# Six landing places for transposed score blocks, one output accumulator, the bias on GpSimd and the first masks on ScalarE, in the attention stage of a four-stage graph kernel

## The chip, the core and the metric

The kernel runs on one core of a Trainium2 chip. Its time is the device time of one execution in microseconds. The kernel before took 1704.58 us, the median of three runs (1696.35, 1704.58 and 1709.76). Engines are named as in the profile: PE is TensorE, PEld its weight loads, DVE is VectorE, ACT is ScalarE, POOL is GpSimd, SP is SyncE; SPq, ACTq and POOLq are the instructions with which these engines issue DMAs.

## What is computed

The input x has 3327 rows of 256 numbers, adj is a 3327 by 3327 matrix of zeros and ones. Four blocks follow one another, each added to x: an attention over the graph, a mixture of 8 experts with two chosen per row, a graph convolution, and a second mixture of experts. The change lies in the first block and in the projections ahead of it:

```python
def _L0_gnn_ref(x, adj, weight, bias, node_w, edge_w):
    node_att = jax.nn.softmax(x @ node_w, axis=0)
    h = x @ edge_w
    e = h @ h.T
    e = jnp.where(adj > 0, e, NEG_BIG)
    edge_att = jax.nn.softmax(e, axis=1)
    combined_att = node_att * edge_att
    support = x @ weight
    output = adj * combined_att @ support
    return output + bias
...
x = x + _L0_gnn_ref(_layernorm(x, axis=-1), adj, ...)
```

The product h h^T is symmetric, and both kernels use that.

## The kernel before, in words

Rows are worked on in tiles of 128, 26 of them (T = 26, padded to 3328 rows). Every engine has its own instruction stream, written out by hand tile by tile, and the streams meet at semaphores (`wait_ge`, `then_inc`). Nothing reorders them.

**Projection** (`project`). For each tile t, DVE normalises the rows (L511), PE transposes them (L564), ACT copies the transpose out (`copy_t`, L542), and PE multiplies by weight and node_w (L574) and by edge_w (L579). ACT then writes the high part of each product (support L550, h_t L551), and DVE the low part, the rest after rounding (L523, L525). All large products are kept as such pairs, high and low, and a product is formed from three partial products: high by high, high by low, low by high. In this stage SP also loads the first two rows of tiles of adj into one place ADJ (`adj_tile`), and POOL makes from each an additive mask, 0 or minus a large number, for tiles 0 and 1 (L492).

**Attention** (`attend`). For tile t:

- *Scores.* PE forms 7 chunks of up to 512 columns in an order (`ORDER`) that begins with the chunk of the tile itself. A chunk on or right of the diagonal is computed from `attn_h_tile` (HS, the tile's slice of h_t that POOL copies, L737) and h_t by six matmuls (L921). Those right of the diagonal are also copied out by ACT (L768) and stored to DRAM by SP (`raw_scores`, L658), and a chunk left of the diagonal is not computed: SP loads the stored block (L669) to one of `TURN_SLOTS` places and PE transposes it in four pieces (L916). Tile t has t // 4 such turned chunks, so five in tiles 20 to 23 and six in tiles 24 and 25. A place may be loaded again when PE has transposed what was in it: `load_scores(m)` waits for block m - `TURN_SLOTS`. DVE adds the mask and takes the maximum of each chunk (L828), which frees one of the four score banks. DVE is in order: in tile t's step its first five L828 of tile t + 1 stand ahead of the first two L811 of tile t.
- *Softmax.* ACT takes the exponential over the whole row tile (L781).
- *Output product.* PE transposes the probabilities (L930) in groups of four blocks; ACT writes their high part (L791), DVE the low part (L811). For each of 26 blocks PE multiplies the high part by support's high and low part at once, 512 columns (L956, L961 in the last block), and the low part by support's high part, 256 columns (L958). The left half of the bank holds two partial products, the right half one.
- *Tail.* DVE adds the bias to x (L865), adds the right half (L869), adds the left half (L872), and takes statistics (L226, L231). POOL normalises the new rows (L245 to L257), and a small gate is computed among the next tile's work.

PE's stream in step t is: scores of tile t + 1 with the first transposes of tile t set in after the fifth chunk, then the output product of tile t.

SP's stream in step t is: load adj for tile t + 1 (when POOL has made the mask out of ADJ, L742), store the output of tile t - 2 (L650), store its neighbour's normalised rows (L261), load x of tile t (L701), store kept chunks (L658), load turned chunks (L669), both for coming use.

ACT issues the first expert's weights for the next stage (`first_w_in`, `first_w_out`, L775 and L776) at tile 3; their places FIRST and FIRST_OUT are not read before the expert stage.

## Time and profile before

| what | value |
|---|---|
| time, median of 3 runs | 1704.58 us (1696.35 to 1709.76) |
| time of the profiled execution | 1700.52 us |
| its span, first to last instruction | 1698.7 us |
| granted clock of TensorE, mean | 0.949 |
| PE busy | 1480.6 us, 87% of the span |
| DVE, ACT, POOL busy | 1025.2, 660.3, 811.4 us |
| projection stage, about | 0 to 88 us of the span |
| attention stage, about | 89 to 650 us of the span |

The profiled execution lies 1.8 us outside its span (1700.52 against 1698.7) and 4.1 us below the median of the three runs. The busy time of PE counts instructions that overlap by their drain: the time from the start of one matmul to the start of the next is shorter than the duration of one. Shares over the whole span mix stages that have different limits, so places are read from the timeline, where the idle time ahead of an instruction and what ended it stand in square brackets.

### The profile page before, as it was taken

The numbers are of one execution on the slowest core, as the hardware profiler recorded it, in microseconds if no ns is written. First come the engines' busy times: TensorE is split into PE (matmuls) and PEld (weight loads), VectorE is DVE, ScalarE is ACT, GpSimd is POOL, SyncE is SP. The second block draws the span as 40 slices with busy tenths as digits, with TensorE's granted clock in tenths as the row PEclk, the third lists the DMA queues.
The fourth block names the chain that finished last, engine by engine and source line by source line (L and its number), as shares of the span: only waits on it lengthen the run. The fifth ranks groups of instructions, "written<-read, shape, count | busy, mean of one in ns | idle before, by whom it ended". The sixth has DMA issues, their size and how long they took to land. (4 is left out here: it accounts for less than half of the span.)

```text
span 1698.7 us, 35416 instructions
## 1 busy us (share of the span) xinstructions
PE 1480.6 (87%) x9072; PEld 1243.8 (73%) x9072; DVE 1025.2 (60%) x3475; ACT 660.3 (39%) x1483; POOL 811.4 (48%) x1578
## 2 busy tenths in 40 slices
PE   5889999999999874999989917899949999999994
PEld 4768788888888763778877804455538888888894
DVE  5546566677776664555565454677756655666652
ACT  2334444444443331222222332111125565555562
POOL 1013444444544424666666612688844445545551
PEclk8999999999999996999999969899969999999997
DMA  5056667666776522663323367888526632222223
GB/s 194 0 181 209 217 208 231 225 223 229 241 249 209 171 75 79 151 140 58 49 49 46 50 146 166 164 173 173 113 85 155 161 75 37 37 37 37 37 39 97
DMA packets 247532, 221.57 MB, mean 130 GB/s; under 512 B 120363, under 2 KB 226729, under 8 KB 243929
## 3 DMA queue, kind: packets, MB, share of 16 engines
q1 hardware_dynamic: 213784, 161.71, 34.2%
q0 software_dynamic: 25984, 31.06, 11.3%
q10 hardware_dynamic: 7680, 27.84, 4.4%
q8 instruction: 33, 0.54, 0.1%
q14 instruction: 51, 0.42, 0.1%
HBM read 127.29 MB, written 74.52 MB: 119 GB/s over the span
## 5 line engine op out<-in xcount | busy, mean ns | idle before, releaser
L1167 PE MATMUL bank<-ffn_w_in_parts,ffn_x_t 128*128 128x512 f32 x1416 | 363.1, 404 | 17.3 <-DVE ffn_x_t L1283 14.2
L1167 PEld LDWEIGHTS bank<-ffn_w_in_parts,ffn_x_t 128*128 128x128 f32 x1416 | 259.0, 190 | 77.1 <-DVE ffn_x_t L1283 17.5
L1191 PE MATMUL bank<-ffn_w_out_parts,ffn_hidden_t 128*128 128x256 f32 x2124 | 284.5, 288 | 16.8 <-DVE ffn_hidden_t L1290 16.5
L1191 PEld LDWEIGHTS bank<-ffn_w_out_parts,ffn_hidden_t 128*128 128x128 f32 x2124 | 262.9, 192 | 22.4 <-issue 15.8
L956 PE MATMUL bank<-support,attn_probs_t 128*128 128x512 f32 x650 | 254.8, 424 | 11.9 <-DVE attn_probs_t L811 11.6
L1131 POOL DMA_INDIRECT x<-ffn_y,ffn_dst x118 | 192.4, 1631 | 55.1 <-issue 52.8
L1486 PE MATMUL bank<-normed_parts,nbr_adj_t 128*128 128x512 f16 x676 | 161.6, 385 | 41.0 <-DVE nbr_adj_t L1605 36.0
L1233 ACT ACTIVATE ffn_silu_or_gelu<-bank,w_b_in 128x128 f32<-128x128 f32 x472 | 134.6, 368 | 145.2 <-PE bank L1178 145.2
L791 ACT CAST attn_probs_t<-bank 128x512 fp32r<-128x512 f32 (+1 forms) x182 | 98.9, 559 | 235.4 <-PE bank L930 233.2
L958 PE MATMUL bank<-support,attn_probs_t 128*128 128x256 f32 x676 | 188.9, 286 | 0.0
L811 DVE TENSOR_TENSOR attn_probs_t<-bank,attn_probs_t 128x512 fp32r<-128x512 f32 (+1 forms) x182 | 116.2, 651 | 96.5 <-ACT attn_probs_t L791 91.1
L1290 DVE TENSOR_TENSOR ffn_hidden_t<-ffn_silu_or_gelu,ffn_hidden_t 128x512 fp32r<-128x512 f32 x118 | 80.6, 692 | 126.2 <-ACT ffn_hidden_t L1239 120.1
L956 PEld LDWEIGHTS bank<-support,attn_probs_t 128*128 128x128 f32 x650 | 126.3, 194 | 38.7 <-issue 11.3
L828 DVE CUSTOM_DVE_ANT_0 attn_scores<-bank,attn_mask 128x512 f32<-128x512 f32 (+1 forms) x182 | 113.4, 649 | 57.8 <-PE bank L921 38.9
L921 PE MATMUL bank<-h_t,attn_h_tile 128*128 128x512 f32 (+1 forms) x660 | 143.1, 372 | 4.1 <-POOL attn_h_tile L737 4.1
L1486 PEld LDWEIGHTS bank<-normed_parts,nbr_adj_t 128*128 128x128 f16 x676 | 65.0, 101 | 107.2 <-issue 40.7
L921 PEld LDWEIGHTS bank<-h_t,attn_h_tile 128*128 128x128 f32 x660 | 117.4, 190 | 27.4 <-issue 4.2
L245 POOL TENSOR_TENSOR attn_rstd<-attn_mean_var,attn_constants 128x1 f32<-128x1 f32 x26 | 4.9, 188 | 272.6 <-DVE attn_mean_var L231 272.6
L958 PEld LDWEIGHTS bank<-support,attn_probs_t 128*128 128x128 f32 x676 | 131.6, 195 | 1.2
L1120 POOL DMA_INDIRECT ffn_x_gathered<-xn,ffn_tok x118 | 123.5, 1047 | 17.2 <-issue 1.2
L930 PE MATMUL bank<-attn_identity,attn_scores 128*128 128x128 f32 x676 | 102.4, 278 | 1.5 <-ACT attn_scores L781 1.5
L1130 POOL TENSOR_TENSOR ffn_wait_taker<-ffn_identity 128x1 f32<-128x1 f32 x118 | 23.3, 198 | 157.6 <-DVE ffn_y L1341 126.2
(274 smaller groups left out, 2561.0 us busy)
## 6 DMA issues: line engine op xcount, KB each, us to landing
adj_tile<-in_adj SPq DMA_DIRECT2D x25, 1663.5 KB
mask<-attn_mask ACTq DMA_DIRECT2D x26, 832.0 KB, 3.4
attn_scores_to_turn<-raw_scores SPq DMA_DIRECT2D x72, 256.0 KB
...
```

The source lines that it names most:

```text
L811: dve.tensor_tensor(PT[:, half(slot, g), 1, 0:gn * P], bank[4 + half(slot, g)][:, 0:gn * P], PT[:, half(slot, g), 0, 0:gn * P].bitcast(F32 ...
L828: dve.tensor_tensor_reduce(out=SC[:, slot, c0:c0 + cn], in0=bank[k % 4][:, 0:cn], in1=NEG[:, slot, c0:c0 + cn], scale=1.0, scalar=-3.0e38, ...
L921: ins = pe.matmul(bank[k % 4][:, 0:cn], HS[:, slot, hs, kd, :], HT[:, hm, kd, c0:c0 + cn], start=n == 0 and kd == 0, stop=n == 2 and kd == ...
L930: ins = pe.transpose(bank[4 + half(slot, g)][:, j * P:(j + 1) * P], SC[:, slot, (g0 + j) * P:(g0 + j + 1) * P], ID[:])
L956: pe.matmul(bank[6 + slot][:, :], part[:, 0, :], SUP[:, jt, :, :].rearrange("p a d -> p (a d)"), start=jt == 0, stop=False)
L958: ins = pe.matmul(bank[6 + slot][:, 0:D], part[:, 1, :], SUP[:, jt, 0, :], start=False, stop=False)
L1120: pool.indirect_dma_start(out=XG[:, slot, :], out_offset=None, in_=a["xn"], in_offset=bass.IndirectOffsetOnAxis(ap=TOKS[:, slot:slot + 1], ...
L1131: pool.indirect_dma_start(out=acc, out_offset=bass.IndirectOffsetOnAxis(ap=DSTS[:, slot:slot + 1], axis=0), in_=YS[:, slot, :], in_offset= ...
L1167: ins = pe.matmul(bank[2 + 2 * slot + b][:, :], XT[:, slot, xp, k, :], WIP[:, wp, k, b * CH:(b + 1) * CH], start=n == 0 and k == 0, stop=n ...
L1191: ins = pe.matmul(bank[7][:, 0:D], HTT[:, hp, k, :], WOP[:, wp, k, :], start=n == 0 and k == 0, stop=n == 2 and k == KH - 1)
L1233: ins = act.activation(GATE[:, j, k * P:(k + 1) * P], src[:, k * P:(k + 1) * P], ACT.Gelu, bias=w.BI[:, bass.ds(e * KH + (4 * j + k), 1)])
L1486: ins = pe.matmul(bank[2 + slot][:, :], AT[:, slot, g0 + j, :], XH[:, g0 + j, :, :].rearrange("p a d -> p (a d)"), start=g0 + j == 0, stop ...
```

## The change

It does six things.

1. `TURN_SLOTS` goes from 4 to 6. The places are no longer a tile of their own: they are FIRST (four places of 512 columns) and FIRST_OUT (two). So the first expert's weights can't be loaded until the last scores are formed, and their load moves from tile 3 to the last tile, behind `act.wait_ge(qk_done, T * NC)`.
2. The output product of one block is three matmuls of 256 columns into the same half bank, where it was one of 512 and one of 256 into a whole bank. DVE's L869 goes.
3. The addition of the bias moves from DVE (L865) to POOL (`add_bias`), and SP waits for it before it loads x again into the same place.
4. The masks of tiles 0 and 1 are made by ACT in the projection stage, as an activation over 3328 columns at tiles 17 and 23, where POOL made them. The second load of adj waits for the first mask as before, and so comes later.
5. POOL copies the h slices of tiles 0 and 1 in the projection stage, and PE waits for neither at the start of the attention.
6. The node softmax on POOL stands ahead of the tile steps; its small tiles have places of their own.

```diff
@@ -68,7 +68,7 @@
 ORDER = [list(range(t // 4, NC)) + list(range(t // 4)) for t in range(T)]
 KEPT = [(t, c) for t in range(T) for c in ORDER[t] if c > t // 4]
 TURNED = [(t, c) for t in range(T) for c in ORDER[t] if c < t // 4]
-KEEP_SLOTS, TURN_SLOTS = 3, 4
+KEEP_SLOTS, TURN_SLOTS = 3, 6
...
@@ -442,6 +443,7 @@
         projected, hi_ready, lo_ready = s.sem("projected"), s.sem("hi_ready"), s.sem("lo_ready")
 
         AT_STEP = {1: 1, 8: 2}
+        MASK_AT = {17: 0, 23: 1}
         with nc.Block(no_gpsimd_drain=True) as block:
             @block.sync
             def _(sp):
@@ -449,6 +451,7 @@
                 load_nodes(sp, X, a["x"], arrived)
 
                 sp.wait_ge(arrived[-1], 48)
+                sp.wait_ge(edge, 1)
                 sp.dma_start(a["ADJ"][:, 0:N], a["adj"][0:P, :]).then_inc(adj_in, 16)
                 sp.wait_ge(mask_made, 1)
                 sp.dma_start(a["ADJ"][:, 0:N], a["adj"][P:2 * P, :]).then_inc(adj_in, 16)
@@ -484,12 +487,13 @@
...
-
                 pool.memset(a["ADJ"][:, N:NP], 0.0).then_inc(edge, 1)
-                pool.wait_ge(edge, 1)
+                pool.memset(MINUS[:], -BIG).then_inc(edge, 1)
+
                 for t in range(2):
-                    pool.wait_ge(adj_in, (t + 1) * 16)
-                    pool.tensor_scalar(a["NEG"][:, t, :], a["ADJ"][:], BIG, -BIG, ALU.mult, ALU.add).then_inc(mask_made, 1)
+                    pool.wait_ge(lo_ready, (t + 1) * 2)
+                    pool.tensor_copy(a["HS"][:, t, :, :, :].rearrange("p a k n -> p (a k) n"),
+                                     HT[:, :, :, t * P:(t + 1) * P].rearrange("p a k n -> p (a k) n").bitcast(F32))
 
             @block.vector
             def _(dve):
@@ -546,6 +550,12 @@
                     slot = t % 2
                     if t + 1 < T:
                         copy_t(t + 1)
+                    if t in MASK_AT:
+
+                        m = MASK_AT[t]
+                        act.wait_ge(edge, 2)
+                        act.wait_ge(adj_in, (m + 1) * 16)
+                        act.activation(a["NEG"][:, m, :], a["ADJ"][:], ACT.Identity, bias=MINUS[:], scale=BIG).then_inc(mask_made, 1)
...
@@ -592,16 +602,18 @@
     HT, SUP, NL = a["HT"], a["SUP"], a["NL"]
     with ExitStack() as ctx:
         s = Stage(nc, ctx, "attn")
-
-        TURN = s.sb("scores_to_turn", [P, TURN_SLOTS, CH])
-        NATT, VAL, NSM = NL, TURN[:, 0, 0:T], TURN[:, 0, T:T + 4]
+        NATT, VAL, NSM = s.sb("node_attention", [P, T]), s.sb("valid", [P, T]), s.sb("node_small", [P, 4])
+
+        TURN = [v[:, i:i + CH] for v in (a["FIRST"][:].rearrange("p k m -> p (k m)"), a["FIRST_OUT"][:].rearrange("p k d -> p (k d)"))
+                for i in range(0, v.shape[1], CH)]
+        assert len(TURN) == TURN_SLOTS
...
-        HS = s.sb("h_tile", [P, 2, 2, KD, P], F32R)
+        HS = a["HS"]
...
@@ -694,6 +706,8 @@
                         store(t - 2, slot)
                     if t >= 3:
                         gate.store(sp, t - 3, 1 - slot)
+                    if t >= 2:
+                        sp.wait_ge(x_ready, t - 1)
...
@@ -729,25 +743,38 @@
                     pool.wait_ge(e_ready, 1)
                     pool.partition_all_reduce(NSM[:, 3:4], NSM[:, 2:3], P, RADD).then_inc(sum_all, 1)
 
+                def add_bias(t):
+
+                    slot, uses = t % 2, t // 2
+                    pool.wait_ge(x_in[slot], (uses + 1) * 16 + (16 if t == T - 1 else 0))
+                    if t >= 2:
+                        pool.wait_ge(x_out[slot], uses * 16)
+                        pool.wait_ge(gate.normed, t - 1)
+                    pool.tensor_tensor(XO[:, slot, :], XB[:, slot, :], BB[:], ALU.add).then_inc(x_ready, 1)
+
                 def step(t, uses, slot, first, last):
-                    if not known(t) or t >= 3:
+                    if t >= 3:
                         gate.norm(pool, t - 3, uses - 2 + slot, 1 - slot)
+                    if t >= 1:
+                        add_bias(t - 1)
                     if not first:
                         pool.wait_ge(masked, (t - 1) * NC)
-                    pool.tensor_copy(HS[:, slot, :, :, :].rearrange("p a k n -> p (a k) n"),
-                                     HT[:, :, :, bass.ds(t * P, P)].rearrange("p a k n -> p (a k) n").bitcast(F32)).then_inc(h_ready, 1)
+                        pool.tensor_copy(HS[:, slot, :, :, :].rearrange("p a k n -> p (a k) n"),
+                                         HT[:, :, :, t * P:(t + 1) * P].rearrange("p a k n -> p (a k) n").bitcast(F32)).then_inc(h_ready, 1)
                     if not first:
                         pool.wait_ge(adj_in, (t - 1) * 16 + (16 if last else 0))
                         pool.wait_ge(mask_out[slot], uses * 16)
                         pool.tensor_scalar(NEG[:, slot, :], ADJ[:], BIG, -BIG, ALU.mult, ALU.add).then_inc(mask_ready, 1)
-                    if first and slot == 1:
-                        node_softmax()
                     if t >= 4:
                         gate.scatter(pool, t - 4, uses - 2, slot)
                 gate.constants(pool)
+                node_softmax()
+                pool.wait_ge(bias_in, 16)
                 unrolled(T, step)
                 for t in range(T - 3, T):
                     gate.norm(pool, t, t // 2, t % 2)
+                    if t == T - 3:
+                        add_bias(T - 1)
                     gate.scatter(pool, t - 1, (t - 1) // 2, (t - 1) % 2)
...
@@ -771,7 +798,8 @@
                     if first and slot == 0:
                         act.wait_ge(nmx_ready, 1)
                         act.activation(NATT[:], NL[:], ACT.Exp, bias=NSM[:, 1:2], accum_out=NSM[:, 2:3]).then_inc(e_ready, 1)
-                    if known(t) and t == 3:
+                    if last:
+                        act.wait_ge(qk_done, T * NC)
                         act.dma_start(a["FIRST"][:], a["w_in"][0][:, :, 0:2 * H0]).then_inc(first_in, 16)
                         act.dma_start(a["FIRST_OUT"][:], a["w_out"][0][:, :, 0:D]).then_inc(first_in, 16)
...
@@ -858,17 +886,9 @@
                     dve.wait_ge(factor, t * 2 + 1)
                     dve.scalar_tensor_tensor(SM[:, slot, 5:6], SM[:, slot, 4:5], SM[:, slot, 3:4],
                                              NATT[:, bass.ds(t, 1)], ALU.mult, ALU.mult).then_inc(factor, 1)
-                    dve.wait_ge(x_in[slot], (uses + 1) * 16 + (16 if last else 0))
-                    if not first:
-                        dve.wait_ge(x_out[slot], uses * 16)
-                        dve.wait_ge(gate.normed, t - 1)
-                    dve.tensor_tensor(XO[:, slot, :], XB[:, slot, :], BB[:], ALU.add).then_inc(x_ready, 1)
                     dve.wait_ge(factor, t * 2 + 2)
                     dve.wait_ge(pv_group, (t + 1) * NG)
                     dve.wait_ge(x_ready, t + 1)
-                    dve.scalar_tensor_tensor(XO[:, slot, :], bank[6 + slot][:, D:2 * D], SM[:, slot, 5:6],
-                                             XO[:, slot, :], ALU.mult, ALU.add).then_inc(out_part, 1)
-                    dve.wait_ge(out_part, t + 1)
                     dve.scalar_tensor_tensor(XO[:, slot, :], bank[6 + slot][:, 0:D], SM[:, slot, 5:6],
                                              XO[:, slot, :], ALU.mult, ALU.add).then_inc(out_ready, 1)
...
             @block.tensor
             def _(pe):
                 def scores(t, slot, first, midway=None):
-                    pe.wait_ge(h_ready, t + 1)
+                    if t >= 2:
+                        pe.wait_ge(h_ready, t - 1)
...
@@ -952,14 +972,9 @@
                         for j in range(gn):
                             jt = g0 + j
                             part = PT[:, half(slot, g), :, j * P:(j + 1) * P]
-                            if jt < T - 1:
-                                pe.matmul(bank[6 + slot][:, :], part[:, 0, :], SUP[:, jt, :, :].rearrange("p a d -> p (a d)"),
-                                          start=jt == 0, stop=False)
-                            ins = pe.matmul(bank[6 + slot][:, 0:D], part[:, 1, :], SUP[:, jt, 0, :],
-                                            start=False, stop=False)
-                            if jt == T - 1:
-                                ins = pe.matmul(bank[6 + slot][:, :], part[:, 0, :], SUP[:, jt, :, :].rearrange("p a d -> p (a d)"),
-                                                start=False, stop=True)
+                            for n, (hp, hs) in enumerate([(0, 0), (0, 1), (1, 0)]):
+                                ins = pe.matmul(bank[6 + slot][:, 0:D], part[:, hp, :], SUP[:, jt, hs, :],
+                                                start=jt == 0 and n == 0, stop=jt == T - 1 and n == 2)
                         ins.then_inc(pv_group, 1)
...
@@ -1717,6 +1732,7 @@
             a["FIRST_OUT"] = layer.enter_context(nc.sbuf_tensor("first_w_out", [P, H0 // P, D], F32))
             with ExitStack() as keep:
                 a["ADJ"] = keep.enter_context(nc.sbuf_tensor("adj_tile", [P, NP], F32))
+                a["HS"] = keep.enter_context(nc.sbuf_tensor("attn_h_tile", [P, 2, 2, KD, P], F32R))
```

PE, within one group of the output product (`support` is the value operand, `attn_probs_t` the transposed probabilities). Before:

```order
L930 MATMUL bank<-attn_identity,attn_scores 128x128 x4
L956 MATMUL bank<-support,attn_probs_t 128x512
L958 MATMUL bank<-support,attn_probs_t 128x256
L956 MATMUL bank<-support,attn_probs_t 128x512
L958 MATMUL bank<-support,attn_probs_t 128x256
L956 MATMUL bank<-support,attn_probs_t 128x512
L958 MATMUL bank<-support,attn_probs_t 128x256
L956 MATMUL bank<-support,attn_probs_t 128x512
L958 MATMUL bank<-support,attn_probs_t 128x256
```

and now:

```order
L950 MATMUL bank<-attn_identity,attn_scores 128x128 x4
L976 MATMUL bank<-support,attn_probs_t 128x256 x12
L950 MATMUL bank<-attn_identity,attn_scores 128x128 x4
L976 MATMUL bank<-support,attn_probs_t 128x256 x12
L282 MATMUL bank<-attn_gate_w,attn_x_normed_t 128x8 x2
```

The eight matmuls of a group, 3072 columns in all, are twelve with the same number of columns; the place of the transposes is the same.

SP, the steps around the first tile with five turned chunks. Before:

```order
L658 DMA raw_scores<-attn_scores_kept 128x2x128
L669 DMA attn_scores_to_turn<-raw_scores 128x512 x4
L692 DMA adj_tile<-in_adj 128x3327
L650 DMA x<-attn_x_out 128x256
L261 DMA xn<-attn_x_normed 128x256
L701 DMA attn_x<-in_x 128x256
L658 DMA raw_scores<-attn_scores_kept 128x2x128
L669 DMA attn_scores_to_turn<-raw_scores 128x512 x5
```

and now:

```order
L670 DMA raw_scores<-attn_scores_kept 128x2x128
L681 DMA first_w_out<-raw_scores 128x512 x2
L681 DMA first_w_in<-raw_scores 128x512 x3
L704 DMA adj_tile<-in_adj 128x3327
L662 DMA x<-attn_x_out 128x256
L261 DMA xn<-attn_x_normed 128x256
L715 DMA attn_x<-in_x 128x256
L670 DMA raw_scores<-attn_scores_kept 128x2x128
```

Before, four blocks of the next tile are loaded a step ahead and the fifth stands in the step that needs it; now all five are loaded a step ahead.

ACT, the start of the last tile's step. Now:

```order
L819 CAST attn_probs_t<-bank 128x256
L803 DMA first_w_in<-in_w 128x2x1024
L804 DMA first_w_out<-in_w 128x4x256
L807 DMA mask<-attn_mask 128x3328
L809 ACTIVATE attn_scores,attn_small<-attn_scores,attn_small 128x3328
```

Before, the two loads of the first weights stood at this place of tile 3's step, and the last tile's step had only the store of the mask ahead of the exponential.

## Rows read from the trace of the kernel before

**Rows 1.** Busy time by stretch: PE, PEld, DVE, ACT, POOL (counts), granted clock, DMA share, GB/s

```profile
400.00:500.00 100.00, 97.79 (x646) 86.89 (x645) 74.33 (x319) 46.44 (x71) 46.74 (x95) 1.00 0.70 238
```

**Rows 2.** Waits in the attention: engine, line, waited for: us in total, times, longest

```profile
PE bank L916 <- DVE attn_max L828: 7.2, 5, 2.1
PE bank L916 <- DMA attn_scores_to_turn<-raw_scores: 7.1, 3, 2.9
```

**Rows 3.** Timeline of SP's queue, stores of the tiles' outputs: start, us, queue, line

```profile
173.22 0.34 SPq L650 DMA_DIRECT2D x<-attn_x_out  x1
...
200.52 0.34 SPq L650 DMA_DIRECT2D x<-attn_x_out  x1
...
221.63 0.34 SPq L650 DMA_DIRECT2D x<-attn_x_out  x1
...
496.05 0.34 SPq L650 DMA_DIRECT2D x<-attn_x_out  x1
...
515.07 0.34 SPq L650 DMA_DIRECT2D x<-attn_x_out  x1
...
619.49 0.34 SPq L650 DMA_DIRECT2D x<-attn_x_out  x1
```

**Rows 4.** Timeline of PE, late attention: start, us, line, count, [idle before <-releaser]

```profile
501.33 0.63 PE L916 MATMUL bank<-attn_identity,attn_scores_to_turn 128*128 128x128 f32 x4 [1.88 <-DMA attn_scores_to_turn<-raw_scores]
520.60 0.63 PE L916 MATMUL bank<-attn_identity,attn_scores_to_turn 128*128 128x128 f32 x4 [2.12 <-DVE attn_max L828]
```

**Rows 5.** Busy time by stretch, right behind the second of these gaps

```profile
520.60:523.60 3.00, 3.00 (x14) 2.67 (x15) 1.07 (x6) 0.00 (x0) 2.68 (x5) 0.65 0.72 221
```

**Rows 6.** Timeline of ACT, tile 3's exponential, behind three DMA issues

```profile
171.87 3.08 ACT L781 ACTIVATE attn_scores<-attn_scores,attn_small 128x3328 f32<-128x3328 f32 x1 [1.64 <-issue]
```

**Rows 7.** DMA issues: KB each, us from issue to landing

```profile
first_w_in<-in_w ACTq DMA_DIRECT2D x1, 1024.0 KB, 6.2
```

**Rows 8.** Groups by line: busy us, mean ns | idle before

```profile
L865 DVE TENSOR_TENSOR attn_x_out<-attn_x,attn_bias 128x256 f32<-128x256 f32 x26 | 10.9, 419 | 0.0
...
L869 DVE SCALAR_TENSOR_TENSOR attn_x_out<-bank,attn_small,attn_x_out 128x256 f32<-128x256 f32 x26 | 12.6, 484 | 4.0 <-PE bank L961 0.7
...
L257 POOL TENSOR_SCALAR attn_x_normed<-attn_x_out,attn_rstd 128x256 f32<-128x256 f32 x26 | 14.5, 558 | 0.0
```

**Rows 9.** Timeline of PE in an output-product group: second block, and what follows the fourth

```profile
448.18 0.40 PE L956 MATMUL bank<-support,attn_probs_t 128*128 128x512 f32 x1
...
449.23 0.60 PE L930 MATMUL bank<-attn_identity,attn_scores 128*128 128x128 f32 x4
```

**Rows 10.** Timeline of PEld: weight loads of the experts' 256-column matmuls, back to back

```profile
1430.36 2.94 PEld L1191 LDWEIGHTS bank<-ffn_w_out_parts,ffn_hidden_t 128*128 128x128 f32 x24
```

**Rows 11.** The same weight loads as a group by line

```profile
L1191 PEld LDWEIGHTS bank<-ffn_w_out_parts,ffn_hidden_t 128*128 128x128 f32 x2124 | 262.9, 192 | 22.4 <-issue 15.8 <-DVE ffn_hidden_t L1290 6.2
```

**Rows 12.** Timeline of ACT, DVE and PE in the projection stage, tiles 22 to 25

```profile
81.61 0.39 ACT L542 COPY proj_normed_t<-bank 128x256 f32<-128x256 f32 x1
...
82.22 0.41 DVE L511 TENSOR_SCALAR proj_normed<-proj_x,proj_mean_var 128x256 f32<-128x256 f32 x1
82.86 0.38 PE L564 MATMUL bank<-proj_identity,proj_normed 128*128 128x128 f32 x2
83.06 0.37 ACT L550 CAST support<-bank 128x256 fp32r<-128x256 f32 x1 [1.06 <-PE bank L579]
...
84.83 1.03 PE L574 MATMUL bank<-proj_weight_node,proj_normed_t 128*128 128x257 f32 x4
```

**Rows 13.** Timeline of POOL: the second mask, and how long it waited for adj

```profile
33.23 2.97 POOL L492 TENSOR_SCALAR attn_mask<-adj_tile 128x3328 bf16<-128x3328 f32 x1 [7.41 <-DMA adj_tile<-in_adj]
```

**Rows 14.** Timeline at the start of the attention

```profile
89.28 0.29 POOL L719 TENSOR_SCALAR_AFFINE_SELECT attn_identity<-attn_identity 128x128 f32<-128x128 f32 x1
...
90.82 2.41 PE L921 MATMUL bank<-h_t,attn_h_tile 128*128 128x512 f32 x6 [4.06 <-POOL attn_h_tile L737]
```

**Rows 15.** Timeline of PE behind the last tile's exponential

```profile
619.72 1.09 PE L930 MATMUL bank<-attn_identity,attn_scores 128*128 128x128 f32 x8 [1.54 <-ACT attn_scores L781]
```

18 lines of the change are left out of this document (9 added, 9 removed).

## The prediction, made before the changed kernel ran

> **What bounds the kernel now.** I read the busy time by stretch first, for the limit of the stage that is changed. In the middle of the attention PE is busy 97.8 of 100 us at full granted clock (1.00, the 2.4 GHz level), DVE 74, ACT and POOL under 47, and the DMA engines 70% at 238 GB/s [rows 1]. So there a term counts only if it is PE's own time, or lets PE wait. Next I read the waits, for PE's. The turned chunks (L916) account for two of them: 7.2 us in 5 waits put down to DVE and 7.1 us in 3 put down to the load of turned blocks [rows 2]. Third, the stores of the tiles' outputs, since the distance between two is the length of one tile's step [rows 3]: 19.02 us from 496.05 to 515.07, then 104.42 us for five steps (515.07 to 619.49), 20.9 each, although each holds less work for PE. Steps 19 and on are the first in which tiles 20 to 25, with five and six turned chunks, are scored. The gaps stand in PE's timeline [rows 4].
>
> **Six places.** With four places the fifth block of a tile can be loaded only when PE has transposed the first of the same tile. The gap at 501.33 is that, 1.88 us. The one at 520.60 (2.12 us) is put down to DVE, but it has the same place in the step and nearly the same length; I read it as the same load. Behind it the granted clock is 0.65 over 3 us [rows 5], after PE had stood; behind the 1.88 us no such loss appears. What a clean step would last comes from the first: 19.02 - 1.88 = 17.14 us. With six turned chunks one chunk of six 512-column matmuls, about 0.23 us each by the pair cost below, gives way to four transposes of about 0.45 us together (0.63 with their drain [rows 4]), so 0.9 us less: 16.2 us. The six steps lose 1.88 + (104.42 - 3 x 17.14 - 2 x 16.2) = 1.88 + 20.6 = 22.5 us, of which the clock is a third.
> All blocks are now loaded one step ahead, and the wait for the place is for the block six back. What is late next is DVE: five L828 and one L811 must be done before the output product starts, and L811 also waits for ACT's L791. I put 0.3 us of new gap in each step, 1.7 us in all. Gain: 20.8 us. Bounds: 14 us, if DVE's wait takes a gap of over 1 us in each step; 22.5 if none.
>
> **The first weights.** Their load at tile 3 (1.5 MB) meets the stores of kept chunks and the load of adj: the step that ends at 200.52 takes 27.30 us, the next 21.11 [rows 3]. Both hold the same scores but for one chunk's place. Gone: 6.2 us, bounds 3.5 and 6.2. At their new place ACT issues both ahead of the last exponential. At tile 3 this held ACT 1.64 us [rows 6]. PE waits for the last exponential already, 1.54 us [rows 15], so all 1.64 us add to a wait that becomes 3.2 us, and gaps that long have cost about 1.5 us of clock more (the step at 520.60: 20.9 - 17.14 - 2.12). Cost 3.1 us, bounds 1.6 and 3.3. Landing takes 6.2 us [rows 7] and has the whole last step as cover; without it the next stage would start later by the rest.
>
> **Bias and tail.** DVE loses L865 and L869, 0.419 + 0.484 = 0.9 us a tile [rows 8]. In most steps PE doesn't wait for DVE, so of 23.5 us nearly nothing shows: 0.5 us in the steps up to 19, and the 0.48 us of L869 behind the very last product. In the late steps it is what keeps the new gap at 0.3 us. Gain 1.0 us, bounds 0 and 3. POOL gains an addition of 128x256: between 0.56 us (L257, one operand) and twice that, since it reads two; it stands between the normalisation and the copy of h. POOL is under half busy [rows 1], and the sum of a tile is needed more than a step later. If that cover were gone, DVE would stand at the tail in every tile by what is missing. The mask and the next adj load move back by the same 0.6 to 1.1 us. SP's new wait is for an addition done a step before.
>
> **One accumulator.** Columns are the same, matmuls are 3 in place of 2. From 448.18, the second block of a group, to 449.23, the transposes behind the fourth, PE issues three blocks [rows 9], so 0.350 us a block. What a 256-column matmul with its own weight load costs is seen in the experts: 24 loads in 2.94 us, the last lasting 0.19, so (2.94 - 0.19) / 23 = 0.1196 us from one to the next [rows 10, 11]. Three make 0.359 us, 0.009 more than now; 26 x 26 blocks give +6.0 us, all on PE. Bounds: 0, if a third matmul costs its columns alone, and +10.
> The Trainium skill ("TensorE: Matmul & The Clock Gate", Back-to-back issue gap) states N / 2.4 + 2.5 ns for an isolated matmul; by that the third instruction would cost 2.5 ns and this term +1.7 us; rows 9 and 10, at the same clock, show larger gaps and decide.
>
> **First masks and h slices.** ACT waits 1.06 us per tile for PE in the projection. A mask is an activation over 3328 columns like the exponential, 3.08 us [rows 6]. Behind `copy_t`, which ends at 82.00, it lasts to 85.1 where ACT would start L550 at 83.06: 2.0 us late [rows 12]. Tile 17 has the same pattern; there the lateness goes through DVE to its normalisation of a later tile, which is ready at 82.63 for a transpose at 82.86, a slack of 0.2: PE stands 1.8 us. At tile 23 no normalisation is left; the copy for tile 25, one step of 2.0 us behind the one that ends at 82.00 and 2.0 late, is there at 86.0, where its matmul began at 84.83: 1.2 us. Cost 3.0 us, bounds 2 and 4. The second load of adj needed 7.4 us [rows 13] and has 10.6 us of cover (from the end of the first mask, six steps ahead of 85.1, to 82.0 + 1.8); if it were later, ACT would wait for the rest. At the start of the attention PE no longer waits for the h slices but for the identity, ready at 89.57 in place of 90.82 for the first matmul [rows 14]: gain 1.2 us. The node softmax is bound by the same waits as before: nothing.
>
> **Sum.** -20.8 - 6.2 - 1.0 - 1.2 = -29.2; +3.1 + 6.0 + 3.0 = +12.1; together -17.1 us. The profiled execution took 1700.5 us, so it would be 1683.4; the median of before is 4.1 us higher, and the forecast goes by the median: 1704.6 - 17.1 = 1687.5 us. Less than 1% (17.0 us) is about what can't be told from no change here.
>
> **Rivals.**
> *A: the third weight load is not hidden.* Loads last 192 ns [rows 11], longer than the 107 ns in which 256 columns stream at full clock. If a load were exposed in full, a 256-column matmul would cost 0.19 us and a block 0.58: +0.226 x 676 = 153 us, 1834 us. The rest of the change gives 29.2 - 6.1 = 23.1 us, 0.034 a block, so this decides from (0.350 + 0.034) / 3 = 0.128 us a matmul on, and makes it slower by 1% from 0.136 on. Rows 10 speak against it: 0.1196 with a different weight in each.
> The Trainium skill (same page, Measured speedup vs the span model) says of packed matmuls that a weight load overlaps a running matmul only when the row group differs; by that, with its 128 / 1.2 = 107 ns a load, a block would cost 0.65 us against 0.54 as an estimate, +74 us; rows 10 disagree, and I give it 2 in 100 within this rival. Chance of A together: 0.04.
> *B: the waits move.* The late steps become bound by DVE: seven L828 and two L811 stand between the tail and the start of the product. For it: PE's gap at 520.60 is put down to DVE. Against it: DVE has 26% of idle time, and gets 0.9 us a tile. Then the six places give 12 us and the rest stays: 1696 us. Chance 0.22.
> *C: the sum without the price of the third matmul*, a block costing as before, and the masks mostly hidden: -17.1 - 6.0 - 2 = -25, 1680 us. For it: in rows 9 the gap per instruction is nearly that small. Chance 0.20.
> *D: the change doesn't do what it says at tile 3*: the step is long for another reason (adj and kept chunks alone), or POOL's additions collide with the late adj load. Then 6.2 us stay: 1694 us. Chance 0.10.
> The forecast: 0.44.
>
> **Numbers.** The range takes in B, C and D and the spread of three runs: 1676 to 1701 us. Faster by over 1% means below 1687.5: half of the forecast's case (0.21), nearly all of C (0.19), a little of D and B: 0.45. Slower by over 1%: A and mishaps in the projection: 0.06. The same: 0.49.
>
> **What would show it.** Stores of outputs 17.4 and 16.5 us apart in the last six steps, no L916 wait over 0.5 us put down to DMA, granted clock near 1 there; a step of 21 us at tile 3; in the product twelve matmuls of a group in 1.43 us plus the entry; two PE gaps of 1.8 and 1.2 us in the projection; a gap of 3.2 us before the last exponential's transposes. It is wrong if blocks of the product cost over 0.37 us, if PE waits over 1 us for L828 or L811 in late steps, or if the step at tile 3 stays at 27 us.

## The result, and the profile after

The changed kernel takes 1687.4 us (median of 4 runs, 1685.0 to 1690.5) where the kernel before takes 1702.2 beside it (median of 4, one run more than in the table above). The record's ratio of the runs is 0.9898 (95% interval 0.9866 to 0.993); it is not the quotient of the two medians, which is 0.9913. Measured again beside two of the experiments the changed kernel gave 1687.7 us beside 1706.6, and a ratio of 0.9901 (0.9872 to 0.9929). So it is faster, by about 1%: both intervals leave out no change at all, and both reach to a gain of only 0.7%. The forecast was 1687.5.

The profiled execution took 1686.9 us, with a span of 1685.2 and a mean granted clock of 0.953. Busy time by stretch, the same 100 us as in [rows 1]:

```profile
400.00:500.00 100.00, 97.91 (x791) 94.19 (x790) 69.28 (x301) 43.78 (x70) 52.96 (x97) 1.00 0.72 241
```

PE is as full as before with more matmuls, DVE 5 us emptier, POOL 6 us busier. The longest waits of PE in the attention's product stage (engine, line, waited for: us, times, longest), to be read against [rows 2]:

```profile
PE bank L976 <- DVE attn_probs_t L839: 11.5, 20, 4.3
PE bank L950 <- ACT attn_scores L809: 3.1, 1, 3.1
```

No wait for turned chunks (L936 now) is left. The stores of outputs, as in [rows 3]:

```profile
171.21 0.34 SPq L662 DMA_DIRECT2D x<-attn_x_out  x1
192.39 0.34 SPq L662 DMA_DIRECT2D x<-attn_x_out  x1
...
489.99 0.34 SPq L662 DMA_DIRECT2D x<-attn_x_out  x1
507.83 0.34 SPq L662 DMA_DIRECT2D x<-attn_x_out  x1
...
595.71 0.36 SPq L662 DMA_DIRECT2D x<-attn_x_out  x1
616.00 0.33 SPq L662 DMA_DIRECT2D x<-attn_x_out  x1
```

Tile 3's step is 21.18 us (27.30 before), the six late ones 17.84 four times and 17.18 twice (105.7 in all, 123.4 before), and the last 20.29 (16.15 before). Where PE stood twice, with the low clock behind [rows 4, 5], it is now busy throughout:

```profile
515.00:520.00 5.00, 5.00 (x46) 5.00 (x45) 2.02 (x8) 2.13 (x5) 3.98 (x6) 1.00 0.72 230
520.00:525.00 5.00, 5.00 (x46) 4.95 (x45) 3.86 (x18) 2.63 (x4) 0.00 (x0) 1.00 0.66 271
```

PE's timeline, which answers to [rows 9], [rows 12, 14] and [rows 15] in this order:

```profile
424.99 1.68 PE L976 MATMUL bank<-support,attn_probs_t 128*128 128x256 f32 x12
426.51 0.51 PE L282 MATMUL bank<-attn_gate_w,attn_x_normed_t 128*128 128x8 f32 x4
```
```profile
70.28 0.44 PE L574 MATMUL bank<-proj_identity,proj_normed 128*128 128x128 f32 x2 [1.46 <-DVE proj_normed L515]
...
83.28 0.89 PE L584 MATMUL bank<-proj_weight_node,proj_normed_t 128*128 128x257 f32 x3 [0.90 <-ACT proj_normed_t L546]
...
88.14 4.15 PE L941 MATMUL bank<-h_t,attn_h_tile 128*128 128x512 f32 x11 [2.87 <-POOL attn_identity L733]
```
```profile
598.21 1.09 PE L950 MATMUL bank<-attn_identity,attn_scores 128*128 128x128 f32 x8 [3.12 <-ACT attn_scores L809]
600.36 2.90 PE L976 MATMUL bank<-support,attn_probs_t 128*128 128x256 f32 x12 [1.06 <-DVE attn_probs_t L839]
```

Two gaps in the projection stage (1.46 and 0.90 us), the wait for the last exponential at 3.12, and behind it a group of 12 matmuls at nearly half the pace (2.90 us where the group at 424.99 has 1.68; the granted clock is 0.50 from 600.36 us on for 3 us). From one group to the next the product is measured start to start: 1.52 us from 424.99 to the instruction behind the group. Set against the prediction, by place:

| place, us | forecast | measured |
|---|---|---|
| up to the first store of an output | +2.0 | -2.1 |
| tile 3's step | -6.0 | -6.1 |
| steps 1, 2 and 4 to 18 (17 of them) | +3.4 | +2.1 |
| the six late steps | -19.4 | -17.7 |
| the last step | +2.8 | +4.1 |
| to the last store | -17.2 | -19.6 |

(The forecast's product term is spread evenly over the 26 tiles here, and its bias term of -1.0 halved between the 17 steps and the last. Measured: differences of the stores' times in the two profiles.)

The profile of the kernel before shows where tile 3's step lost its time. ScalarE waited 4.22 us for the store of a kept chunk, PE waited 3.49 us behind it, and then ran at half the clock (a row of busy time by stretch, the clock third from the end):

```profile
182.32 0.59 ACT L768 COPY attn_scores_kept<-bank 128x512 f32<-128x512 f32 x1 [4.22 <-DMA raw_scores<-attn_scores_kept]
184.40 0.77 PE L956 MATMUL bank<-support,attn_probs_t 128*128 128x512 f32 x1 [3.49 <-DVE attn_probs_t L811]
184.00:187.00 3.00, 2.60 (x8) 2.25 (x9) 2.19 (x11) 0.16 (x1) 2.41 (x4) 0.50 0.75 199
```

With the load gone the same 3 us in the changed kernel are full, at 1.00. So of the 6.1 us PE's wait is somewhat more than half; the rest, by subtraction, is the clock behind it. Behind the attention the span gets 6.1 of the 19.6 us back: the neighbours' stage, which nothing in the change touches, took 221.1 us of the profile before (first to last of PE's instructions) and 228.5 after.

### The profile page after: what moved, and what is told of

It is laid out like the page before. It is cut to its first block and busy times, and to the rows that moved or that the text cites. A ratio compares the mean times of both kernels' runs of the same rounds, so it can differ in the third digit from the quotient of the medians.

```text
span 1685.2 us, 36741 instructions
## 1 busy us (share of the span) xinstructions
PE 1478.3 (88%) x9748; PEld 1275.2 (76%) x9748; DVE 998.1 (59%) x3423; ACT 664.7 (39%) x1485; POOL 825.4 (49%) x1603
## 5 line engine op out<-in xcount | busy, mean ns | idle before, releaser
L976 PE MATMUL bank<-support,attn_probs_t 128*128 128x256 f32 x2028 | 284.9, 291 | 11.8 <-DVE attn_probs_t L839 11.5
L976 PEld LDWEIGHTS bank<-support,attn_probs_t 128*128 128x128 f32 x2028 | 256.5, 192 | 16.8 <-issue 12.3
L1146 POOL DMA_INDIRECT x<-ffn_y,ffn_dst x118 | 196.1, 1662 | 53.2 <-issue 51.1
L839 DVE TENSOR_TENSOR attn_probs_t<-bank,attn_probs_t 128x512 fp32r<-128x512 f32 (+1 forms) x182 | 116.2, 650 | 92.3 <-ACT attn_probs_t L819 91.9
L1135 POOL DMA_INDIRECT ffn_x_gathered<-xn,ffn_tok x118 | 122.2, 1036 | 17.2 <-issue 1.1
L1193 PE MATMUL bank<-ffn_identity,ffn_hidden 128*128 128x128 f32 x708 | 97.0, 273 | 2.9 <-DVE ffn_hidden L1293 2.1
L1145 POOL TENSOR_TENSOR ffn_wait_taker<-ffn_identity 128x1 f32<-128x1 f32 x118 | 24.7, 210 | 150.0 <-DVE ffn_y L1356 118.7
L1131 POOL COPY ffn_tok<-ffn_pairs 128x1 int32 (+1 forms) x118 | 86.8, 736 | 5.8 <-PE bank L1171 3.7
```

The lines of the kernel that those rows point to most:

```text
L839: dve.tensor_tensor(PT[:, half(slot, g), 1, 0:gn * P], bank[4 + half(slot, g)][:, 0:gn * P], PT[:, half(slot, g), 0, 0:gn * P].bitcast(F32 ...
L976: ins = pe.matmul(bank[6 + slot][:, 0:D], part[:, hp, :], SUP[:, jt, hs, :], start=jt == 0 and n == 0, stop=jt == T - 1 and n == 2)
L1135: pool.indirect_dma_start(out=XG[:, slot, :], out_offset=None, in_=a["xn"], in_offset=bass.IndirectOffsetOnAxis(ap=TOKS[:, slot:slot + 1], ...
L1146: pool.indirect_dma_start(out=acc, out_offset=bass.IndirectOffsetOnAxis(ap=DSTS[:, slot:slot + 1], axis=0), in_=YS[:, slot, :], in_offset= ...
L1193: ins = pe.transpose(h_bank[slot if HB == 1 else j][:, k * P:(k + 1) * P], HH[:, (4 * j + k) * P:(4 * j + k + 1) * P], ID[:])
```

## The experiments

All edits but the first are to the changed kernel. Ratios are to the kernel before on the same chip. "To the first product" is PE's time from the span's start to its first L976-type matmul, "the products' span" is from there to the end of the last. Before they are 115.7 and 518.6 us, after 112.8 and 502.6, and in the second profile of the same kernel 113.1 and 502.7. These two profiles agree to 0.3 us, but others show that a place can differ by more. In five profiles of kernels that are alike up to the first product it starts at 112.8 to 113.8, and the first score matmul at 86.9 to 89.0. Four profiles with the same last step have 18.9, 18.9, 20.1 and 20.3 us for it. The experiments ran on three chips, so kernels of different chips are compared by their ratios and not by their times. One had the six places alone, the four places, the two matmuls and the masks on POOL. The next had the masks in idle time, the weights behind the exponential, the five places for kept scores and the bias. The last had the five places to turn, the four edits together and the changed kernel again.

### The six places alone

```diff
-KEEP_SLOTS, TURN_SLOTS = 3, 4
+KEEP_SLOTS, TURN_SLOTS = 3, 6
...
-        TURN = s.sb("scores_to_turn", [P, TURN_SLOTS, CH])
...
+        TURN = [v[:, i:i + CH] for v in (a["FIRST"][:].rearrange("p k m -> p (k m)"), a["FIRST_OUT"][:].rearrange("p k d -> p (k d)"))
+                for i in range(0, v.shape[1], CH)]
...
-                    if known(t) and t == 3:
+                    if last:
+                        act.wait_ge(qk_done, T * NC)
```

> The kernel before with one part of the change: six places for blocks to turn, which lie in the first weights' place, and the first weights loaded in the last step behind the last key product. The product in two halves, the bias on VectorE and the masks on POOL stay as before. My terms: the waits of TensorE for turned blocks in the last seven steps go (-20.8 us), the load of tile 3 no longer stands in front of the stores (-6.2), the load in its new place costs 3.1; sum -24, so about 1678 us beside 1702, and faster than the whole change (1687) by 9. If instead the rest of the change costs less than I summed (the third matmul less than 6 us, the masks off POOL a gain and not +3.0), this kernel lands at 1683 to 1688, level with the whole change.

Measured: 1682.5 us, ratio 0.9906 (0.989 to 0.9921); the whole change has 0.9898. Products' span 500.5, tile 3's step 21.21, the six late steps 106.2 together (17.7 each), the last 19.93. So this part alone gives all that the change gives within the intervals, and the theory that the rest costs 7 to 9 us falls: the rest nets nothing that can be told. The late steps give 17.2 us, not 20.8; tile 3 gives 6.1 as forecast; the last step costs 3.8. The other 17 steps are 1.4 us longer in all (340.6 beside 339.2), which no run explains. In the two steps with six turned chunks PE now waits for VectorE twice:

```profile
580.69 0.66 PE L918 MATMUL bank<-attn_identity,first_w_in 128*128 128x128 f32 x4 [0.41 <-DVE attn_max L830]
583.86 0.47 PE L958 MATMUL bank<-support,attn_probs_t 128*128 128x512 f32 x1 [0.77 <-DVE attn_probs_t L813]
```

1.2 us, where the four steps before have one wait of 0.44. So these two steps are no shorter than the others, although they hold less work for PE.

### Four and five places

```diff
-KEEP_SLOTS, TURN_SLOTS = 3, 6
+KEEP_SLOTS, TURN_SLOTS = 3, 4
...
-                for i in range(0, v.shape[1], CH)]
+                for i in range(0, v.shape[1], CH)][:TURN_SLOTS]
```

> The changed kernel with four places to turn in instead of six, still in the first weights' place. If the late waits for blocks go by the number of places, TensorE's gaps of 1.9 to 2.9 us at the turned blocks come back in the last seven steps and the time is about 1687 + 20 = 1707 us, while the step of tile 3 stays at 21.2 us. If the waits went because nothing but the load order changed (rival), the steps stay at 17.8 us and the time at 1687.

Measured: 1697.0 us, ratio 0.9996 (0.9981 to 1.0012). PE's waits from 480 to 627 us:

```profile
PE bank L936 <- DMA first_w_in<-raw_scores: 11.0, 6, 3.3
PE bank L950 <- ACT attn_scores L809: 3.1, 1, 3.1
PE bank L976 <- DVE attn_probs_t L839: 0.6, 1, 0.6
```

The waits are back, one in each of the six steps and all put down to the load now, and tile 3's step stays at 21.19: two separate gains. That all six are put down to the load supports the prediction's reading of the gap at 520.60, which the trace of before put down to DVE. But the six steps take 118.0 us, 12.2 over six places, not 20. Their gaps are 1.87, 1.40, 1.15, 1.27, 3.28 and 2.04 us, 11.0 in all, where before has 1.88, 2.12, 2.05, 2.12, 2.75 (two in one step) and 2.90, 13.8 in all. And the clock fell behind three of them, where it fell behind five before. It stayed up behind the second, at the place where [rows 5] showed 0.65, and fell behind the first, where before it stayed up behind a gap of the same length:

```profile
516.50:519.50 3.00, 2.97 (x26) 3.00 (x27) 1.64 (x8) 0.20 (x1) 2.92 (x1) 1.00 0.87 256
498.00:501.00 3.00, 3.00 (x16) 3.00 (x15) 0.43 (x2) 0.86 (x2) 2.46 (x5) 0.50 0.78 206
```

So the first of these steps is 20.78 us where before has 19.02. What shortened the gaps in the middle, with four places in both kernels, must lie in the rest of the change; no run isolates it. And how often the clock falls can be chance: this kernel, as most others here, has one profile.

With `5` in place of `4`:

> The changed kernel with five places to turn in. Theory: a tile waits when it has more blocks to turn than there are places: tiles 20 to 23 have five and their steps stay at 17.8 us (18.5 to 20.8 with four places), tiles 24 and 25 have six and their steps take 19 to 21 us instead of 17.2: +4 us, about 1690 us. Rival: what counts is the time from a place's release to its next use, so that five places still wait a little in every step: the steps of 20 to 23 at 18.2 to 18.6, about 1692.

Measured: 1694.9 us, ratio 0.994 (0.9917 to 0.9963); 7 us over the changed kernel beside it. Steps of 17.84 four times, then 21.32 and 17.94: a tile waits only where it has more blocks than there are places, as the theory had it. PE's waits for blocks are 4.9 us in 2, the longest 3.4; in the profile the last product ends 2.9 us later, the rest of the 7 is not explained.

### The product in two matmuls

```diff
+                    dve.scalar_tensor_tensor(XO[:, slot, :], bank[6 + slot][:, D:2 * D], SM[:, slot, 5:6],
+                                             XO[:, slot, :], ALU.mult, ALU.add).then_inc(out_part, 1)
...
-                            for n, (hp, hs) in enumerate([(0, 0), (0, 1), (1, 0)]):
-                                ins = pe.matmul(bank[6 + slot][:, 0:D], part[:, hp, :], SUP[:, jt, hs, :],
-                                                start=jt == 0 and n == 0, stop=jt == T - 1 and n == 2)
+                            if jt < T - 1:
+                                pe.matmul(bank[6 + slot][:, :], part[:, 0, :], SUP[:, jt, :, :].rearrange("p a d -> p (a d)"),
+                                          start=jt == 0, stop=False)
+                            ins = pe.matmul(bank[6 + slot][:, 0:D], part[:, 1, :], SUP[:, jt, 0, :],
+                                            start=False, stop=False)
...
```

> The changed kernel with the output product as before: a matmul of 512 columns and one of 256 for a block, and VectorE's addition of the right half. Theory: the third matmul costs 0.006 to 0.01 us a block of 26 x 26, 4 to 6 us in all, and VectorE's addition gives at most 0.5 us a tile of it back where VectorE is the later one, so 1682 to 1684 us. Rival: three matmuls of 256 columns cost nothing that sets the end, or the addition on VectorE costs more than they do: 1687 to 1692. The group of 12 matmuls took 1.52 us in the changed kernel; here the group of 8 should take 1.48.

Measured: 1680.4 us, ratio 0.9887 (0.9869 to 0.9906). Products' span 498.1, 4.5 us shorter than after. Two groups of four blocks in this kernel:

```profile
424.76 0.48 PE L979 MATMUL bank<-support,attn_probs_t 128*128 128x512 f32 x1
...
426.26 0.60 PE L953 MATMUL bank<-attn_identity,attn_scores 128*128 128x128 f32 x4
426.62 0.48 PE L979 MATMUL bank<-support,attn_probs_t 128*128 128x512 f32 x1
```

1.50 us for the group and 1.86 from one to the next, where the changed kernel has 1.52 and, from 423.11 to 424.99, 1.88. That is 0.005 us a block, seven groups a tile make 0.14, and the steps bear it out: 21.03 beside 21.19, 20.24 beside 20.37, 19.30 beside 19.44, 18.53 beside 18.70. In the two steps with six turned chunks it is the other way round, 17.53 beside 17.17. There VectorE has no pause over 0.04 us from the first addition behind one product to the start of the next product, and the second addition (0.48 us, and 0.04 to the next instruction) stands in that row: 0.52 us longer for it and about 0.15 shorter for the product. Over all tiles the third matmul is a cost and not a saving, of 3.5 to 4.5 us; by the runs' ratios alone the two kernels can't be told apart.

### The masks: on POOL again, and in ScalarE's idle time

```diff
-        MASK_AT = {17: 0, 23: 1}
+        MASK_AT = {}
...
+                for t in range(2):
+                    pool.wait_ge(adj_in, (t + 1) * 16)
+                    pool.tensor_scalar(a["NEG"][:, t, :], a["ADJ"][:], BIG, -BIG, ALU.mult, ALU.add).then_inc(mask_made, 1)
```

> The changed kernel with the first two masks made on POOL again, in the projection stage, and not on ScalarE. Theory: POOL's pass over 128 x 3328 of SBUF (2.96 us) holds up the VectorE instruction that runs beside it, as at 22.99 us before (2.85 us where it takes 0.17) and at 33.77 (2.58 where it takes 0.41): TensorE's first gap grows from 5.8 to 8.5 us and one of 1.4 comes back, the two gaps for ScalarE (1.46 and 0.90) go; sum +2.5, about 1690 us, and the first score matmul at 90 to 91 us. Rival: VectorE was slow there for the adjacency's load beside it, which runs here as well and ran in the changed kernel: then the two gaps go and nothing comes, about 1685 us, first score matmul at 86.

Measured: 1685.4 us, ratio 0.9928 (0.9914 to 0.9942), whose interval meets the change's. In the trace PE's first gap is 8.36 us and the one of 1.31 is back. POOL's two passes, and the DVE instructions that started within them:

```profile
22.40 2.96 POOL L500 TENSOR_SCALAR attn_mask<-adj_tile 128x3328 bf16<-128x3328 f32 x1 [2.36 <-DMA adj_tile<-in_adj]
33.22 2.97 POOL L500 TENSOR_SCALAR attn_mask<-adj_tile 128x3328 bf16<-128x3328 f32 x1 [7.86 <-DMA adj_tile<-in_adj]
```
```profile
22.66 2.72 DVE L148 TENSOR_TENSOR proj_mean_var<-proj_row_sums 128x10 f32<-128x10 f32 x1
...
33.72 2.61 DVE L519 TENSOR_SCALAR proj_normed<-proj_x,proj_mean_var 128x256 f32<-128x256 f32 x1
```

Both end with POOL's pass (25.38 beside 25.36, 36.33 beside 36.19). In the kernel before it was the next instruction but one that fell into POOL's first pass:

```profile
22.86 2.96 POOL L492 TENSOR_SCALAR attn_mask<-adj_tile 128x3328 bf16<-128x3328 f32 x1 [19.28 <-DMA adj_tile<-in_adj]
```
```profile
22.99 2.85 DVE L150 TENSOR_TENSOR proj_mean_var<-proj_mean_var 128x10 f32<-128x10 f32 x1
```

In the changed kernel, which has no POOL pass there, the same instruction takes

```profile
22.92 0.17 DVE L150 TENSOR_TENSOR proj_mean_var<-proj_mean_var 128x10 f32<-128x10 f32 x1
```

The adj load is not the cause: in the kernel before the first load had landed when POOL's pass began, the second was issued at 25.86, when the slow instruction was over, and no DMA engine moved anything beside it (share 0.00 and 0 GB/s at the end of the row):

```profile
22.90:25.80 2.90, 0.00 (x0) 0.00 (x0) 2.87 (x2) 0.00 (x0) 2.90 (x1) 0.54 0.00 0
```

The Trainium skill ("SBUF — State Buffer", SBUF: two separate sides) calls the port pair that VectorE and GpSimd share a lock, held for the whole instruction, which a VectorE instruction needs if it reads two SBUF inputs or runs in a 2-port mode: the trace agrees for the two-input one, and shows the same of a `tensor_scalar` from SBUF to SBUF.

And yet the first product starts at 113.0 us, 0.1 after the changed kernel's. The first score matmul is 1.6 us later (89.70), but the 72 score matmuls behind it last 15.97 us and not 17.38. The stretch from 89 to 91 us in the changed kernel and in this one, PE first, granted clock third from the end:

```profile
89.00:91.00 2.00, 2.00 (x6) 1.52 (x6) 0.27 (x2) 0.00 (x0) 0.00 (x0) 0.50 0.45 117
```
```profile
89.00:91.00 2.00, 1.30 (x6) 1.10 (x7) 0.73 (x4) 0.00 (x0) 0.97 (x10) 1.00 0.21 57
```

The gap ahead is 2.9 us in both, but in the changed kernel PE had also stood 0.9 us at 83.28 and run in pieces since. The masks on ScalarE spare PE 3.9 us of gaps (8.36 + 1.31 - 5.82) and cost it 2.4 us of new ones and 1.4 us of low clock: nothing is left that can be told. In four other profiles with the same projection the low clock cost more, 18.9 us for the 72 matmuls. So nearly all of the 2.9 us by which the changed kernel is ahead at the first product (115.7 to 112.8) stands in this kernel too, which has the masks on POOL. It is the shorter wait ahead of the first score matmul, for the identity and not for POOL's h copies (2.88 us for 4.06), and the clock behind it: the 72 matmuls took 17.85 us before.

That says where masks should stand: where ScalarE is idle, the first ahead of the third `square_root` (tile 8, and there behind the copies of the tile's products), the second at the attention's start.

```diff
-        MASK_AT = {17: 0, 23: 1}
+        MASK_AT = {8: 0}
...
                 gate.load(act)
+                act.wait_ge(minus, 1)
+                act.activation(NEG[:, 1, :], ADJ[:], ACT.Identity, bias=MINUS[:], scale=BIG).then_inc(mask_one, 1)
```

> The changed kernel with its first two masks on ScalarE, but where ScalarE has nothing to do: the first at 40.4 us, in TensorE's 6.5 us gap for the third span's statistics, the second at the attention stage's start. Theory: the gaps of 1.46 and 0.90 us go, no VectorE instruction is held (the first gap stays 5.8), and the clock stays at 1.00 at the attention's start as in the kernel with POOL's masks (where it fell to 0.50 for 3 us in the changed kernel): first output product at 109.2 us beside 112.8, -3.6 us, 1683 to 1684. Rival: the clock falls in any case behind the gap of 2.9 us, and only 2.4 us go. Second rival: the first product waits for the stores of kept scores, which hide the gain: within 1 us of 1687.

Measured: 1676.8 us, ratio 0.9864 (0.9844 to 0.9884). First product at 107.1 us, 5.7 earlier and not 3.6: both gaps of PE are gone, the first score matmul starts at 83.7, and the 72 behind it last 16.0 us. But some 2 us of this belong to the execution: the two profiles of the last kernel below, whose projection is the same, have their first score matmul at 86.2 and 85.8. Against 88.4 in the profile of the changed kernel beside them that is 2.2 to 2.6 us, and with 1.4 of clock the 3.6 that was expected.

### The first weights behind the exponential

```diff
-                    if last:
-                        act.wait_ge(qk_done, T * NC)
-                        act.dma_start(a["FIRST"][:], a["w_in"][0][:, :, 0:2 * H0]).then_inc(first_in, 16)
-                        act.dma_start(a["FIRST_OUT"][:], a["w_out"][0][:, :, 0:D]).then_inc(first_in, 16)
...
                     act.activation(SC[:, slot, :], SC[:, slot, :], ACT.Exp, bias=SM[:, slot, 0:1],
                                    accum_out=SM[:, slot, 1:2]).then_inc(exp_done, 1)
+                    if last:
+                        act.wait_ge(qk_done, T * NC)
+                        act.dma_start(a["FIRST"][:], a["w_in"][0][:, :, 0:2 * H0]).then_inc(first_in, 16)
+                        act.dma_start(a["FIRST_OUT"][:], a["w_out"][0][:, :, 0:D]).then_inc(first_in, 16)
```

> The changed kernel with the two loads of the first weights issued by ScalarE behind the last exponential instead of ahead of it. Theory: TensorE's gap of 3.12 us at 598.21 holds the two issues (0.63 us each, the exponential begins 1.65 us late), so it falls to about 1.5, and the low clock behind it (the group of 12 matmuls in 2.90 us beside 1.52) may go as well: -1.6 to -3.0 us, 1684 to 1686. Rival: the issues now stand ahead of ScalarE's first copy of turned probabilities, which TensorE waits for 0.5 us later, and half of the gain comes back: -0.8 us, 1686.6. The load itself (6.2 us) is needed some 40 us later and hidden either way.

Measured: 1680.4 us, ratio 0.9867 (0.9843 to 0.9891). The gap and the group behind it:

```profile
597.54 1.09 PE L950 MATMUL bank<-attn_identity,attn_scores 128*128 128x128 f32 x8 [1.49 <-ACT attn_scores L805]
599.69 1.67 PE L976 MATMUL bank<-support,attn_probs_t 128*128 128x256 f32 x12 [1.05 <-DVE attn_probs_t L839]
```

The last step is 15.89 us instead of 20.29, so the place of two issues cost 4.4 us: 1.6 of gap and 2.8 of low clock behind it. The clock's part varies. The kernels with the masks on POOL and in ScalarE's idle time have the same last step with a gap of the same length, and it took 18.9 us in both profiles: 1.4 of clock, 3.0 us in all. The wait of 1.05 that follows is the same in both kernels. It costs no clock here, but the profile of the last kernel's second run has the same two waits (1.54 and 1.06 us) and a clock of 0.50 behind them, for 1.5 us.

### Five places for kept scores

```diff
-KEEP_SLOTS, TURN_SLOTS = 3, 6
+KEEP_SLOTS, TURN_SLOTS = 5, 6
```

> The changed kernel with five places for scores to keep instead of three. Theory: TensorE's gap of 4.33 us ahead of the first output product is ScalarE's wait for a place (5.5 us, from 105.3 to 110.8, released by a store): with two more places it falls to about 1 us, -3 us in all, 1684. Rival: the six stores that SP issues there at 1.06 us each set the pace, and one wait takes the other's place: -1 to 0 us.

Measured: 1675.8 us, ratio 0.9838 (0.9817 to 0.986). ScalarE's wait of 5.5 us for a store is gone and PE's waits for L839 have the pattern

```profile
PE bank L976 <- DVE attn_probs_t L839: 7.3, 20, 0.7
```

PE's gap of 4.33 us ahead of the first product is gone, and not down to 1 us, and so is the low clock behind it. The product starts 21.7 us behind the first score matmul, where the kernel with five places to turn, whose score matmuls ran at the same clock, has 26.2 (24.7 in the changed kernel, whose clock rose sooner). The products' span is 500.0 instead of 502.6. Together that is near 7 us at the last product (608.8 beside 615.4 and 615.9). The two places need 4 KB a partition, and the change gave up a tile of 8 KB; whether the kernel before had room for them without that is not shown.

### The bias on VectorE

```diff
-                    if t >= 1:
-                        add_bias(t - 1)
...
+                    dve.tensor_tensor(XO[:, slot, :], XB[:, slot, :], BB[:], ALU.add).then_inc(x_ready, 1)
```

> The changed kernel with the addition of the bias on VectorE (0.42 us a tile) and not on POOL. Theory: VectorE is what TensorE waits for at the first group of a step in the late tiles (0.4 to 0.7 us), so part of the 0.42 us is added there: 8 to 12 steps by 0.3, +2.4 to +3.6 us, and the tail is 1 us longer: about 1691 us. Rival: it lies in VectorE's idle time in every step, only the tail's 1 us comes: 1688.

Measured: 1684.1 us, ratio 0.9899 (0.9878 to 0.992), products' span 501.6. Most steps are equal to 0.02 us; the two with six turned chunks are 17.40 beside 17.17, and from the first store to the last but one it is 468.9 us beside 468.2 and 468.6 in the two profiles of the changed kernel. The rival holds nearly: with one accumulator the bias on VectorE costs some tenths of a us, most of it in the two steps where PE waits for VectorE longest.

### The four edits together

> The changed kernel with four edits that paid one by one: the product of 512 and 256 columns (attention stage 2.9 us shorter), the first weights' loads behind the last exponential (4.3), the masks where ScalarE is idle (first output product 5.7 earlier), five places for kept scores (the way from first score to first output product 3.0 shorter, and 2 more behind it). Theory, they lie at different places and add up: -18 us against the changed kernel, 1669 us, and the last output product ends at about 597 us of the trace beside 615. Rival: masks and kept scores both worked on the same wait, the first output product, and one of them is worth nothing now: 1673 to 1675.

Measured: 1674.0 us, ratio 0.9811 (0.9784 to 0.9839), 13.7 us or 0.8% under the changed kernel beside it. In the trace the last product ends at 598.5, 17.4 us earlier, close to the sum of 18: the four lie at different places. The first product is 8.2 us earlier (104.97 beside 113.14), which is what the masks (3.6) and the kept scores (4.3) give there. But its neighbours' stage took 232.9 us, and gave 4 to 6 back. The changed kernel beside them, and this one once more:

> The changed kernel once more, beside the others on one chip, so that what they gain is read against it and not only against the kernel before. The ratio was 0.9898 (0.9866 to 0.993); 0.985 to 0.993 here. Of its stages, the neighbours' stage, which the change does not touch and which took 228 us of the trace in the changed kernel's profile beside 221 before, should differ from run to run (221 to 229 in the runs so far) and the projection and attention stages by under 2 us.

> The kernel with the four edits once more, for the length of its stages alone. If the neighbours' stage (232.9 us there, 221 to 230 in the others) varies from one execution to the next, it differs by some us here, and the first 980 us agree within 2. If its length belongs to the kernel, by when its transfers meet, it is 232 to 234 again.

The changed kernel: 1687.7 us, neighbours' stage 227.3, last product at 615.9 (615.4 the first time). The combined one again: one run of 1670.9 beside one of 1697.5, last product at 599.9, neighbours' stage 228.4 us. So of the stage's length 4.5 us at least belong to the execution and not to the kernel. What differs most in it is PE's wait for the lists of pairs: 15.1 us in the profile before, 20.6 after,

```profile
PE bank L328 <- DVE nbr_pairs L322: 23.4, 7, 12.9
```
```profile
PE bank L328 <- DVE nbr_pairs L322: 21.5, 4, 16.0
```

here, the two executions in this order. Over all profiles the stage took 221.1 to 232.9 us. The kernel before has one profile, so whether its 221.1 is more than chance is open; the changed kernel with the masks on POOL has 222.1.

## Why the prediction was right, and where its steps were not

**The total was right, in part by errors of opposite sign.** To the last store the forecast had -17.2 and the traces have -19.6; the neighbours' stage gave some back, and the median moved by -14.7 and, in the second comparison, -18.9. That the time came within 0.1 us of 1687.5 is luck: the forecast started from 1704.6, and the kernel before gave 1702.2 in the comparison.

**Six places: the mechanism right, the size 3.6 us too large.** Waits at turned blocks and the low clock went, and four and five places bring them back where there are more blocks than places. Alone, the six places gave 17.2 us where the term had 20.8. The clean step was mis-sized. 19.02 - 1.88 = 17.14, with 0.3 of new wait, makes 17.4; the first four steps measure 17.7 with the product in halves. The last two, 16.5 with that wait, are 17.7 with the six places alone and 17.2 in the changed kernel. There the term took a turned chunk in place of a computed one for 0.9 us less, by PE's work alone, but PE waits for VectorE, 1.2 us a step with the six places alone and 0.7 in the changed kernel (0.4 in the other steps).

**The first weights: right at the old place (-6.1 for -6.2), too cheap at the new one** (+4.1 for +3.1; 3.0 to 4.4 by the experiment). At the old place the sum took the whole excess of the step and so held the clock's part without naming it. At the new one the gap was forecast at 3.2 and is 3.12; the clock behind it was taken at 1.5 us from the gap at 520.60 and cost 2.8, and 1.4 in two other profiles.

**One accumulator: the sign right, the size too large.** The term said 0.009 us a block, +6.0. The experiment shows 0.005, about +3.5, VectorE's saving already in it. The term was the small difference of two readings: 0.1196 us from one 256-column matmul to the next came from another stage, and 0.350 a block was read off three blocks to 0.01 us, which is 0.003 a block and a third of the difference. Rival A is out: in the changed kernel, too, weight loads of 192 ns on average hide behind the matmuls, 12 of which take 1.52 us, 0.127 each, entry included. The sentence on row groups that rival A takes from the Trainium skill ("TensorE: Matmul & The Clock Gate") stands on that page in the section The mechanism; this trace does not agree with it for these full 128x128 loads.

**Bias on POOL: -1.0 forecast.** With one accumulator it is -0.7 at most. POOL's addition takes 0.73 us, within the forecast's bounds. From the six places alone (which has the bias and both additions on VectorE) to the two-matmul kernel (which has only the additions), the products' span falls by 2.4 us. The bias may be worth that where VectorE has the second addition as well, but the two kernels also differ in masks, h copies and node softmax, so it is not shown.

**Masks and h copies: this step failed.** Forecast +3.0 and -1.2, together +1.8; the traces have about 0 for the masks and -2.8 for the copies at the first product. The gaps were nearly the size forecast (1.46 and 0.90 for 1.8 and 1.2). Missed was that POOL's pass held up VectorE, and PE with it. The row was there: PE's gap of 8.5 us at 28.49 in the timeline before, and ahead of its end a DVE instruction of 10 columns that took 2.85 us; the prediction's rows of the projection's pace start at 81 us. Missed too was the clock at the attention's start: the wait of 4.06 us before had cost 1.9 us behind it, which went with the h copies, and the new gaps cost 1.4 and more.

**Rivals B, C and D.** B (the late steps become bound by VectorE) is true of two steps in six, those with six turned chunks, and small: PE waits 0.7 us there in the changed kernel and 1.2 with the six places alone. In the other four PE waits 0.4 us. C (no price of the third matmul) is half true in size. D is out: tile 3's step is 21.2 us in every kernel that moved the load, with four places too.
